# Row maxima of two heads at a time in two 64-row tiles of TensorE, with values and denominators side by side

## What is computed

```python
qh = (q @ Wq.T + bq).reshape(Bb, Lq, H, hd).transpose(0, 2, 1, 3)
kh = (kv @ Wk.T + bk).reshape(Bb, Lkv, H, hd).transpose(0, 2, 1, 3)
vh = (kv @ Wv.T + bv).reshape(Bb, Lkv, H, hd).transpose(0, 2, 1, 3)
scores = jnp.einsum('bhqd,bhkd->bhqk', qh, kh) * scale
mask = jnp.arange(Lkv)[None, :] <= jnp.arange(Lq)[:, None]
scores = jnp.where(mask[None, None], scores, -jnp.inf)
attn = jax.nn.softmax(scores, axis=-1)
out = jnp.einsum('bhqk,bhkd->bhqd', attn, vh)
```

## Time and profile before

| what | us |
|---|---|
| median of 3 runs | 3473.44 |
| lowest and highest | 3471.66, 3478.7 |
| span of the profiled execution | 3474.1 |
| TensorE busy | 3211.9 (92%) |
| DVE busy | 2010.8 (58%) |
| ACT busy | 1615.1 (46%) |
| POOL busy | 1508.1 (43%) |

### The profile page before, as it was taken

The page is one execution under the profiler, slowest core; times in us unless marked ns, Lnnn a source line. Parts: engine busy times, 40 slices in busy tenths (PEclk is TensorE's granted clock), DMA queues, the critical chain, the costliest instruction groups (busy, mean ns, idle before and its releaser), DMA issues. The chain is left out here.

```text
span 3474.1 us, 48728 instructions
## 1 busy us (share of the span) xinstructions
PE 3211.9 (92%) x16480; PEld 1715.5 (49%) x16480; DVE 2010.8 (58%) x3605; ACT 1615.1 (46%) x2892; POOL 1508.1 (43%) x509
## 2 busy tenths in 40 slices
PE   8967999999999999999999999999784999999997
PEld 6855444443444443444443444443364555666563
DVE  3355787775677775677775677774153233333333
ACT  2122455556555556555556555556421433333332
POOL 1111266675366666356666456667661111111100
PEclk9987899999999999999999999999897999999999
DMA  5456300003200002210002300000288111111000
GB/s 196 159 182 201 81 16 13 13 4 70 65 16 13 13 4 58 65 25 16 13 4 46 77 25 16 4 4 4 66 320 258 37 49 49 49 49 49 25 25 13
DMA packets 108235, 207.88 MB, mean 60 GB/s; under 512 B 9248, under 2 KB 25120, under 8 KB 108000
## 3 DMA queue, kind: packets, MB, share of 16 engines
q1 hardware_dynamic: 88768, 146.04, 14.8%
q0 software_dynamic: 12384, 47.46, 3.5%
q10 hardware_dynamic: 6848, 11.31, 1.0%
HBM read 124.03 MB, written 80.74 MB: 59 GB/s over the span
## 5 line engine op out<-in xcount | busy, mean ns | idle before, releaser
L738 DVE TENSOR_REDUCE row_max<-m_bank 128x1 f32<-128x512 f32 (+3 forms) x2240 | 1292.7, 623 | 486.5 <-PE m_bank L826 387.9
L711 ACT ACTIVATE pT<-s_bank 128x512 f32<-128x512 f32 (+5 forms) x2176 | 1128.1, 570 | 844.1 <-PE s_bank L851 654.2
L659 POOL TENSOR_TENSOR part_sum<-part_sum,pT 128x2048 f32<-128x2048 f32 (+1 forms) x252 | 1140.8, 4527 | 446.5 <-ACT pT L711 436.6
L826 PE MATMUL m_bank<-k_sb,q_sb 96*128 96x512 f32 (+3 forms) x2240 | 908.8, 419 | 50.5 <-DVE row_max L738 27.9
L851 PE MATMUL s_bank<-q_sb,k_sb 104*128 104x512 f32 (+3 forms) x2176 | 888.1, 425 | 15.3 <-ACT pT L711 11.3
L826 PEld LDWEIGHTS m_bank<-k_sb,q_sb 96*128 96x128 f32 x2240 | 436.8, 196 | 443.8 <-DVE row_max L738 350.2
L851 PEld LDWEIGHTS s_bank<-q_sb,k_sb 104*128 104x128 f32 x2176 | 417.7, 194 | 416.2 <-ACT pT L711 334.5
L872 PE MATMUL o_bank<-pT,v_sb 128*32 128x512 f32 (+5 forms) x4352 | 560.8, 587 | 0.0
L659 POOL TENSOR_TENSOR part_sum<-pT 128x2048 f32<-128x2048 f32 x28 | 128.2, 4578 | 438.8 <-ACT pT L711 438.8
L1282 POOL TENSOR_TENSOR f_var_eps<-f_mean_var,eps 128x4 f32<-128x4 f32 x8 | 1.6, 201 | 582.7 <-DVE f_mean_var L1446 582.7
L888 PE MATMUL den_bank<-pT,ones 128*32 128x512 f32 (+5 forms) x1888 | 230.2, 560 | 0.0
(11 more groups left out here) (185 smaller groups left out, 3277.9 us busy)
## 6 DMA issues: line engine op xcount, KB each, us to landing
q_sb<-qT_hi SPq DMA_DIRECT2D x64, 256.0 KB, 4.8
k_sb<-kT_hi SPq DMA_DIRECT2D x48, 256.0 KB, 4.2
x_in<-in_x SPq DMA_DIRECT2D x8, 1024.0 KB, 5.6
qT_hi<-q_hi POOLq DMA_DIRECT2D x8, 1024.0 KB, 4.7
qT_lo<-q_lo POOLq DMA_DIRECT2D x8, 1024.0 KB, 6.7
q_sb<-qT_lo SPq DMA_DIRECT2D x32, 256.0 KB, 4.6
aT<-a_out ACTq DMA_DIRECT2D x32, 256.0 KB, 2.0
a_in<-aT SPq DMA_DIRECT2D x8, 1024.0 KB, 9.5
```

The lines of the kernel that those rows point to most:

```text
L659: pool.tensor_tensor(total, pT[:, (s - 1) % SLOTS, :, q0:] if kt == 1 else total, pT[:, s % SLOTS, :, q0:], ALU.add).then_inc(pool_added, 1)
L711: act.activation(pT[0:rows, s % SLOTS, h, q0:], s_bank[(HG * s + h) % S_RING][0:rows, q0:], ACT.Exp, scale=SCALE).then_inc(exp_done, 1)
L738: dve.tensor_reduce(row_max[:, j % 2, r, h, c:c + 1], m_bank[q % M_RING][:, 0:n], AX_X, ALU.max).then_inc(unit_max, 1)
L826: mm = pe.matmul(out[:, 0:n], q_sb[j % QBUFS][0:R_MAX, h, r * P:(r + 1) * P], k_sb[0:R_MAX, h, c * BLK:c * BLK + n], start=True, stop=not ...
```

## The change

The contraction of a unit falls from 96 rows to 64: q_hi and q_lo against k_hi. The rows are arranged anew in `q_sb` and `k_sb`, so that even heads have these 64 rows on partitions 0 to 63 and odd heads on 64 to 127; the term of k_lo lies in the other half and is read by the score matmuls alone, which now take 104 rows (even heads) or 128 (odd heads, with zero rows that POOL writes once). Two heads then form a pair: two matmuls, one in each half of the rows of the array, to two banks, 280 pairs per group and 1120 in all. DVE takes two maxima of a pair. There are still three banks, now handed out by `SLOT`, and a pair's second matmul waits for the maximum three slots earlier.

The pieces of a step are now scores 0 and 1, values, denominators, scores 2 and 3. Pairs go to two places of a step alone: ahead of the values, and ahead of scores 3. The transposed maxima are copied by two ACT instructions of four times 8 rows instead of one, and loads of queries and keys are six transfers instead of three.

The denominators are no longer copied by ACT. DVE transposes the bank in blocks of 32 by 32, inverts 16 columns, and transposes back with each of them spread over 32; then comes the multiplication. These four stand at the ends of steps 0, 1, 2 and 3 of the next block. In the diff, lines that are only "..." are left out.

```diff
-R_HI, R_MID, R_LO, R_MAX = 0, HD, 2 * HD, 3 * HD
-R_END = R_MAX + 2 * HG
+HALF = P // 2
+BASE = (0, HALF)
+MAX_ROWS = 2 * HG
+R_MAX = (HALF + HD, HD)
+ROWS = (R_MAX[0] + MAX_ROWS, P)
...
-        for h in range(HG):
-            for c in range(key_chunks(j)):
...
+        for c in range(key_chunks(j)):
...
+            for h in range(0, HG, 2):
                 units.append((r, h, c, n, first_masked, masked))
...
+SLOT = [sum(1 if i is None else 2 for _, i in MAX_JOBS[:q]) for q in range(len(MAX_JOBS) + 1)]
...
-PIECES = (0, 1, 2, "values", 3, "denominators")
+PIECES = (0, 1, "values", "denominators", 2, 3)
+JOBS_BEFORE = (2, 5)
...
-            while n < len(jobs) and (when[n] <= at[s][piece] or (s == ST - 1 and piece == len(PIECES) - 1)):
+            while n < len(jobs) and piece in JOBS_BEFORE and (
+                    when[n] <= at[s][piece] or (s == ST - 1 and piece == JOBS_BEFORE[-1])):
...
+                pool.memset(as_f32(k_sb[HD:HALF, 1::2, :]), 0.0).then_inc(const_ready, 1)
+                for buf in q_sb:
+                    pool.memset(as_f32(buf[HD:HALF, 1::2, :]), 0.0).then_inc(const_ready, 1)
...
-                        act.activation(o_sb[:, j % 2], o_bank[:, :], ACT.Copy).then_inc(block_copied, 1)
-                        act.activation(den_sb[:, j % 2], den_bank[:, :], ACT.Copy).then_inc(block_copied, 1)
+                        act.activation(o_sb[:, j % 2], o_bank[:, :], ACT.Copy).then_inc(o_copied, 1)
...
+                        for odd in range(2):
+                            reach(dve, unit_done, 2 * (NU * (g + ahead) + UNITS_BEFORE[j] + i) + odd + 1)
+                            dve.tensor_reduce(row_max[:, j % 2, r, h + odd, c:c + 1], m_bank[(SLOT[q] + odd) % M_RING][:, 0:n],
+                                              AX_X, ALU.max).then_inc(unit_max, 1)
...
-                        dve.reciprocal(rden[:, cols], den_sb[:, j % 2, cols]).then_inc(rden_ready, 1)
+                        dve.transpose(den_cols[:, :], den_bank[:, :]).then_inc(den_taken, 1)
...
+                        dve.reciprocal(rden_col[:, :], den_cols[:, 0:BLK:HD]).then_inc(rden_col_ready, 1)
...
+                        dve.transpose(rden[:, :], rden_col[:, :].unsqueeze(2).to_broadcast([P, BLK // HD, HD])).then_inc(rden_ready, 1)
...
-                        mm = pe.matmul(out[:, 0:n], q_sb[j % QBUFS][0:R_MAX, h, r * P:(r + 1) * P],
-                                       k_sb[0:R_MAX, h, c * BLK:c * BLK + n], start=True, stop=not masked)
...
+                        for odd in range(2):
+                            slot_free(ahead, SLOT[q] + odd)
+                            rows = slice(BASE[odd], BASE[odd] + HALF)
+                            mm = pe.matmul(m_bank[(SLOT[q] + odd) % M_RING][:, 0:n], q_sb[j % QBUFS][rows, h + odd, r * P:(r + 1) * P],
+                                           k_sb[rows, h + odd, c * BLK:c * BLK + n], start=True, stop=not masked)
```

More of the change, by code:

```diff
@@ L496 @@
 MAX_JOBS = max_jobs()
+SLOT = [sum(1 if i is None else 2 for _, i in MAX_JOBS[:q]) for q in range(len(MAX_JOBS) + 1)]
+SLOT_USER = [(j, i, odd) for j, i in MAX_JOBS for odd in range(1 if i is None else 2)]
 FIRST_LEAD = MAX_JOBS.index((0, None)) + 1
@@ L686, in max_to_rows @@
                         reach(act, maxT_done, QB * (g + ahead) + j + 1)
-                        rows = slice(R_MAX, R_END)
-                        bank = m_bank[MAX_JOBS.index((j, None)) % M_RING]
-                        src = bank[rows, :].unsqueeze(1).to_broadcast([R_END - R_MAX, HG, BLK])
-                        act.activation(q_sb[j % QBUFS][rows, :, :], src, ACT.Copy).then_inc(max_rows, 1)
+                        bank = m_bank[SLOT[MAX_JOBS.index((j, None))] % M_RING]
+                        src = bank[R_MAX[0]:R_MAX[0] + MAX_ROWS, :].unsqueeze(1).to_broadcast([MAX_ROWS, HG // 2, BLK])
+                        for odd in range(2):
+                            act.activation(q_sb[j % QBUFS][R_MAX[odd]:R_MAX[odd] + MAX_ROWS, odd::2, :], src, ACT.Copy
+                                           ).then_inc(max_rows, 1)
                     def transposed_maxima(jobs):
@@ L736, in take_max @@
                         r, h, c, n, _, _ = UNITS[j][i]
-                        reach(dve, unit_done, NU * (g + ahead) + UNITS_BEFORE[j] + i + 1)
-                        dve.tensor_reduce(row_max[:, j % 2, r, h, c:c + 1], m_bank[q % M_RING][:, 0:n], AX_X, ALU.max
-                                          ).then_inc(unit_max, 1)
+                        for odd in range(2):
+                            reach(dve, unit_done, 2 * (NU * (g + ahead) + UNITS_BEFORE[j] + i) + odd + 1)
+                            dve.tensor_reduce(row_max[:, j % 2, r, h + odd, c:c + 1], m_bank[(SLOT[q] + odd) % M_RING][:, 0:n],
+                                              AX_X, ALU.max).then_inc(unit_max, 1)
                         if i == len(UNITS[j]) - 1:
@@ L814, in job, with pair @@
                         else:
[L815 to L817 removed]
+                            pair(ahead, q, j, i)
+                    def pair(ahead, q, j, i):
                         r, h, c, n, first_masked, masked = UNITS[j][i]
                         if i == 0:
[L821 removed]
+                            reach(pe, q_loaded[j % QBUFS], 16 * LOADS * (QB // QBUFS * (g + ahead) + j // QBUFS + 1))
@@ L822, in unit @@
                         if c == j and r == 0 and h == 0:
-                            reach(pe, k_loaded[c], 48 * (g + ahead + 1))
-                        bank_free(ahead, q)
-                        out = m_bank[q % M_RING]
-                        mm = pe.matmul(out[:, 0:n], q_sb[j % QBUFS][0:R_MAX, h, r * P:(r + 1) * P],
-                                       k_sb[0:R_MAX, h, c * BLK:c * BLK + n], start=True, stop=not masked)
-                        if masked:
-                            mm = pe.matmul(out[:, first_masked:n], ident_b[:, :], mask[:, 0:masked], start=False, stop=True)
@@ L830, in unit @@
-                        mm.then_inc(unit_done, 1)
+                            reach(pe, k_loaded[c], 16 * LOADS * (g + ahead + 1))
+                        for odd in range(2):
+                            slot_free(ahead, SLOT[q] + odd)
+                            rows = slice(BASE[odd], BASE[odd] + HALF)
+                            mm = pe.matmul(m_bank[(SLOT[q] + odd) % M_RING][:, 0:n], q_sb[j % QBUFS][rows, h + odd, r * P:(r + 1) * P],
+                                           k_sb[rows, h + odd, c * BLK:c * BLK + n], start=True, stop=not masked)
+                            if not masked:
+                                mm.then_inc(unit_done, 1)
@@ L832, in transpose_max @@
+                        for odd in range(2) if masked else ():
+                            pe.matmul(m_bank[(SLOT[q] + odd) % M_RING][:, first_masked:n], ident_b[:, :], mask[:, 0:masked],
+                                      start=False, stop=True).then_inc(unit_done, 1)
                     def transpose_max(ahead, q, j):
                         reach(pe, neg_ready, 3 * (QB * (g + ahead) + j + 1))
-                        bank_free(ahead, q)
+                        slot_free(ahead, SLOT[q])
@@ L850, in scores @@
                         out = s_bank[n % S_RING]
-                        mm = pe.matmul(out[:, q0:], k_sb[0:R_END, h, kt * P:(kt + 1) * P],
-                                       q_sb[j % QBUFS][0:R_END, h, q0:], start=True, stop=kt < 4 * j)
+                        mm = pe.matmul(out[:, q0:], k_sb[0:ROWS[h % 2], h, kt * P:(kt + 1) * P],
+                                       q_sb[j % QBUFS][0:ROWS[h % 2], h, q0:], start=True, stop=kt < 4 * j)
                         if kt >= 4 * j:
```

134 lines of the change are left out of this document (76 added, 58 removed).

## The result

The changed kernel takes **3794.7 us** (median of 4 runs, 3775.7 to 3811.5) against 3472.9 of the kernel before beside it (3471.7 to 3478.7): 1.092 times as long, interval 1.087 to 1.097. It is slower by 322 us where 143 were forecast, and it lies outside the range given.

A forecast was written before the change was run, and what follows sets the result against it. TensorE was taken as the bound, busy 513 of 535 us. Terms +43 - 66 + 16 + 184 - 28 - 25 + 17 + 4 - 2 gave +143, so 3617 us, range 3415 to 3740.

The forecast's parts named there:

- part 1: Pairs in stage `attend`: 235 us of matmul streams saved, but switches to and from the 64-row shape cost more; +43 us.
- the ring: Three banks, a pair takes two: TensorE waits for DVE's maxima at double places, +184 us; earlier waits replaced, -28.
- the hand-over's pairs: From block to block, a pair's two maxima queue on DVE where one did: 0.6 us in 28 places, +17 us.
- the start: Start of the stage: DVE's head rows wait for POOL's zeroing of k_sb and end at 334, +4 us.
- the third rival: The halves of a pair do not run at once, so the 235 us are not saved: 3807 us, chance 0.07.
- the first rival: A 64-row tile is no change of shape, so its switches cost nothing: 3416 us, chance 0.18.
- Part 2: Values next to denominators: a round trip of tile shape saved in 236 steps, -66 us; block 7's steps without pairs, +16.
- Part 3: Two pairs in a row: the fourth matmul waits for the first's maximum, 0.9 us per place, 228 places, +184 us.
- Part 4: DVE's small work: two transposes and a short reciprocal replace eight reciprocals per block; credited -25 us (between -64 and +30).
- Part 5: Start and end of the stage: POOL's zeroing delays DVE's head rows, +4 us; the last block's end gains, -2 us.

The follow-up runs named there:

- b_den_mid3: Kernel before with only the change's denominators by transposes, and the multiplication in the middle of step 3 instead of its end: 3432.8 us, ratio 0.987.
- b_order_den_mid3: b_den_mid3 with the pieces of a step in the change's order, values next to denominators: 3451.1 us, ratio 0.992 to the kernel before.
- norm_mid: Changed kernel with the multiplication in the middle of step 3 instead of at its end: 3655.1 us, ratio 1.052 to the kernel before.
- b_den_end3: Kernel before with only the change's denominators by transposes, the multiplication at the end of step 3 as in the change: 3544.4 us, ratio 1.018.
- the edit of `negate`: The CAST in `negate` replaced by a second reduction of row_max, on b_den_mid3 (3421.6 us), b_order_den_mid3 (3440.6 us) and norm_mid (3658.3 us).
- short_max: Changed kernel with each of DVE's maxima reading only the first 128 columns of its bank: 3534.8 us, ratio 1.017 to the kernel before.
- norm_late: Changed kernel with the multiplication at the end of step 5, where the kernel before has it: 3695.0 us, ratio 1.062 to the kernel before.
- its control: Kernel before with DVE's maxima over the first 128 columns alone: 3414.7 us, ratio 0.981.
- b_den_neg: b_den_mid3 with the CAST in `negate` replaced by a second reduction of row_max: 3421.6 us, ratio 0.985 to the kernel before.
- norm_mid_neg: norm_mid with the CAST in `negate` replaced by a second reduction of row_max: 3658.3 us, ratio 1.052 to the kernel before.

## Why the prediction was wrong

The runs split the 322 us into four parts that the prediction's terms can be held against, each the difference of two kernels along one path: before, b_den_mid3, b_order_den_mid3, norm_mid, after. Another path would share the same total out otherwise: without pairs, the place of the multiplication costs 112 us (b_den_end3 against b_den_mid3) and not 140.

| part | forecast | measured |
|---|---|---|
| pairs: part 1, the ring, the hand-over's pairs, the start | 43 + 184 - 28 + 17 + 4 = +220 | +204 (+218 with the edit of `negate`) |
| order of values and denominators | -66 + 16 = -50 | +18 (+19) |
| transposed denominators, well placed | -25 - 2 = -27 | -45 |
| the multiplication's new place | not priced | +140 |
| sum | +143 | +317 of 322 (the runs of the kernel before differ by 5 us between the rounds) |

**Part 1** was right in the prices that can be read. A pair's halves start together (the third rival, 3807 us, is out although the time lies near it), the next score comes 0.43 us after a pair (1184.33 to 1184.76), and of three scores and the step into the pair there are 0.90 us (1184.76 to 1185.66), which is 0.34 + 0.23 + 0.33. So 64 rows are a change of shape, and the first rival is out. That all of "pairs" came out at 204 us, near the 220, is partly luck: the ring cost somewhat more than its 184 (below), and the hand-over, where the pairs were to cost 17 us more, had 17 us less of waiting. The Trainium skill, "TensorE: Matmul & The Clock Gate", Part 3, has row tiles starting within some 4 ns; the trace agrees.

**Part 2** had the wrong sign. The round trip was saved (some 0.17 us of its 0.28 by the medians of the steps), and block 7 came out at 2.68 and 3.53 us, where 2.71 and 3.58 stood. The first step that failed is that I let the rest of the order cost nothing outside block 7. I worked out that scores 2 and 3 now follow the values, but not what that does at the hand-over, where the negated maxima come late anyway. In the kernel before, the transposes already waited for DVE there (waits view, 400 to 2400 us):
```profile
PE m_bank L837 <- DVE row_max L738: 32.9, 18, 2.8
...
PE m_bank L837 <- DVE neg_parts L753: 10.3, 5, 5.1
```
I credited the saving and did not ask which wait takes it up. Why the order lengthens these waits, from 42 to 60 us, stays open. A second wait stood at nothing as well: ahead of the values, for ACT's copy of `o_sb`, 7 us here and 11.8 in the kernel after.

**Part 3** was right in mechanism and price: 1.24 us forecast from the first to the fourth matmul, 1.28 measured, in 204 to 207 waits where some 200 were expected. The idle time of the waits view is smaller than the forecast (101 us in norm_mid), since a matmul counts as busy until its result is out. In distances from start to start the 159 wide double places of norm_mid lie 171 us above their 0.34, where 143 stood. That the ring makes up most of the cost of the pairs is the sum's reading of this; short_max takes only part of its wait away.

**Part 4** holds the failed step that cost most. I priced the transposes (0.6, measured 0.71 and 0.70), the short reciprocal and the saved 64 us, and the new place of the multiplication not at all: I never asked what `normalise` lands beside at the end of step 3. The trace of before had the answer in one row, which I read wrongly. I used the mean of the multiplication, "the 1.73 us of L768", as the worst price of a transpose. It is no price: the same operation takes 0.68 us in other blocks. The timeline of before shows what the rest is:
```profile
939.91 4.56 POOL L659 TENSOR_TENSOR part_sum<-part_sum,pT 128x2048 f32<-128x2048 f32 x1
...
943.39 1.64 DVE L768 TENSOR_TENSOR a_out<-o_sb,rden 128x512 f32<-128x512 f32 x1
```
It begins 1.08 us before POOL's addition ends and lasts 0.56 beyond it. At the end of step 5 it mostly caught the tail of an addition; at the end of step 3 it catches the head, all 4.5 us, in 13 blocks. That is the 140 us of the table, counted from the best place; counted from the old one (norm_late) it is 100. The Trainium skill, "SBUF — State Buffer", "Who interferes with whom", states that DVE and GpSimd share a port pair which is an exclusive lock held for the whole instruction, and that a DVE operation with two SBUF inputs contends for it with a GpSimd one that reads SBUF. By that rule 0.68 becomes up to 0.6 + 4.5 = 5.1; the trace agrees (5.05), in both directions.

The same part has a size off: with the multiplication well placed the denominators gave 45 us and not 27. The range I had named, down to -64, held that, but part of the 45 is the better place of the multiplication, which I had not counted.

**Part 5.** The first matmul of the stage starts at 337.08, not at 334: the memset of `k_sb` took 5.6 us instead of 6.8, but a second memset, of `q_sb`, that I had not priced runs beside DVE's casts, and these take 10.52 us instead of 7.30. The first values start at 379.5 us; 366.7 before. So the start costs about 13 us and not 4, part of it at half clock (68 us there instead of 58).

**The clock** was in my range and not in my sum. The values above took 1.86 us at 1.2 GHz instead of 1.00. If all work stretches so, 375 us at half clock instead of 99 are up to some 127 of the 322 us, by my estimate. All prices of the sum were read at full clock. norm_mid gives back 187 us at half clock, so up to some 86 of its 140. What waits on TensorE is thus dearer than its own length: behind the stall of 3.50 us another 12.5 us ran at half clock, up to 6 us more. A term "waits times what they cost afterwards" would have put the forecast of the ring higher too, though the other terms hid that.

**What stays open.** What makes short_max better than norm_mid by 57 us beyond its control: the waits saved (65 us less ahead of the units) and the half clock (72 us less) are not taken apart. The edit of `negate` takes 4 to 5 us off TensorE's waits with pairs and without; why the half clock falls by 24 us without pairs (b_den_neg, 11 us faster) and not at all with them (norm_mid_neg, no faster) I can't say. Whether b_den_neg would gain more with the subtraction moved off POOL's additions was not tried. Which stalls are followed by half clock and which are not I can't tell from these traces.

## What to carry to other kernels

A moved instruction is priced by what runs beside its new place, on the other engines, and a mean duration that is a multiple of the shortest one of the same form is a wait and no price: look at single instances before using it. A pair of matmuls that fills two banks at once halves a ring, so count the ring in pairs against the latency of the one who empties it, before counting streams saved. A saving at one wait is worth what the next wait leaves of it, and a stall of TensorE of some microseconds is often paid a second time at half clock.

## What the hardware showed that I had not expected

- Multiplication on DVE and addition on POOL, both with two operands in SBUF, exclude each other for a whole instruction, in either direction: 5.05 us for 0.68 on DVE, or 5.12 for 4.57 on POOL. It holds for 16 columns too (3.16 us for 0.18), and for a CAST of 16 columns from float32 to bfloat16 in SBUF (up to 4.5 us for 0.18, in b_order_den_mid3). Reductions with one operand in SBUF (0.27) or in PSUM do not wait.
- Which of the two wins can't be told from starts 0.02 us apart: POOL's record begins first in both kinds of block (1057.66 and 1664.74), and DVE loses in the one and wins in the other. So such a kernel has blocks of both kinds in one execution.
- Memsets on POOL of 32x1024 took 2.2 us each, and casts on DVE beside them 2.6 instead of 1.8.
